# Low-rank adapter layer in float32: the left operand's rows put together by small SBUF transfers instead of a third transpose, with three steps reordered

## The reference, cut to what matters

```python
# x (2048, 1024); W_base (1024, 1024); A (16, 1024); B_user, B_item (1250, 1024, 16); W_common (1024, 16)
base = x @ W_base.T + b_base
a = x @ A.T                                       # (2048, 16)
user_part = einsum('bor,br->bo', B_user[user_indices], a)
item_part = einsum('bor,br->bo', B_item[item_indices], a)
common_part = a @ W_common.T
return base + 2.0 * (user_part + item_part + common_part)
```

## Time and profile before

| | us |
|---|---|
| runs | 217.42, 219.17, 219.26; median 219.17 |
| profiled execution, its time | 220.41 |
| its span, first to last instruction | 218.8 |
| PE busy | 207.4 |
| DVE busy | 167.3 |
| POOL busy | 73.6 |
| ACT busy | 57.4 |

### The profile page before, as it was taken

One profiled execution on the slowest core, in us unless ns is written; L12 is line 12 of the kernel. 1 busy time (PEld: TensorE's weight loads), 2 busy tenths in 40 slices (PEclk: granted clock), 3 DMA queues, 4 the chain that ended last, 5 costly groups with the idle time before them and its releaser, 6 DMA issues.

```text
span 218.8 us, 3157 instructions
## 1 busy us (share of the span) xinstructions
PE 207.4 (95%) x1176; PEld 180.6 (83%) x1176; DVE 167.3 (76%) x254; ACT 57.4 (26%) x95; POOL 73.6 (34%) x81
## 2 busy tenths in 40 slices
PE   7998999999997999999999999999999999999970
PEld 7787889888876989978889788988888888788870
DVE  1796899467799989999999999669995899136420
ACT  3688443331701232034101142036011400000000
POOL 6002181004052632415365164405441420178020
PEclk9999999999999999999999999999999999999997
DMA  6999969609859997788989989973899884226872
GB/s 196 381 413 402 265 208 319 261 1 252 360 162 318 353 321 267 269 304 311 316 300 298 366 317 258 380 283 123 298 307 366 332 306 173 99 71 217 192 133 63
DMA packets 14673, 57.77 MB, mean 264 GB/s; under 512 B 3812, under 2 KB 4196, under 8 KB 10668
## 3 DMA queue, kind: packets, MB, share of 16 engines
q0 software_dynamic: 7344, 35.30, 49.0%
q1 hardware_dynamic: 7024, 21.73, 27.8%
q10 hardware_dynamic: 288, 0.52, 0.7%
HBM read 58.95 MB, written 11.01 MB: 320 GB/s over the span
## 4 chain that ended last, share of the span: by engine, by line
PE 68%; DVE 16%; DMA 7%; SPq 3%; issue 1%; ACT 1%; DVEq 0%
PE main_ps L1082 17%; PE main_ps L1084 17%; PE main_ps L1083 17%; DVE acc L759 10%; DMA w_lo_raw<-w_t 5%; PE ps_a L1022 3%; PE main_ps L1152 3%; PE ps_a L1023 3%; PE ps_a L1024 3%; DMA x_lo_raw<-x_t 3%; DVE x_lo L655 2%; SPq L301 1%; PE main_ps L1145 1%; SPq L304 1%; PE main_ps L1123 1%
## 5 line engine op out<-in xcount | busy, mean ns | idle before, releaser
L759 DVE SCALAR_TENSOR_TENSOR acc<-rows,a_entry,acc 128x1024 f32<-128x1024 f32 x75 | 96.3, 1284 | 5.5 <-DMA rows<-table,fetch 3.5
L407 POOL DMA_INDIRECT rows<-table,fetch x40 | 54.0, 1349 | 100.8 <-DVE acc L759 90.6
L1082 PE MATMUL main_ps<-w_hi,x_hi 128*128 128x512 f32 (+1 forms) x224 | 83.9, 374 | 0.0
L1084 PE MATMUL main_ps<-w_hi,x_lo 128*128 128x512 f32 (+1 forms) x224 | 82.9, 370 | 0.0
L1083 PE MATMUL main_ps<-w_lo,x_hi 128*128 128x512 f32 (+1 forms) x224 | 82.7, 369 | 0.0
L1083 PEld LDWEIGHTS main_ps<-w_lo,x_hi 128*128 128x128 f32 x224 | 42.1, 188 | 5.5
L1082 PEld LDWEIGHTS main_ps<-w_hi,x_hi 128*128 128x128 f32 x224 | 42.1, 188 | 5.4
L1084 PEld LDWEIGHTS main_ps<-w_hi,x_lo 128*128 128x128 f32 x224 | 42.1, 188 | 4.8
L655 DVE TENSOR_TENSOR x_lo<-x_lo_raw,x_hi 128x1024 fp32r<-128x1024 f32 (+2 forms) x19 | 19.9, 1054 | 0.3
L536 ACT ACTIVATE out_sb<-main_ps 128x912 f32<-128x912 f32 x12 | 11.1, 930 | 33.1 <-PE main_ps L1084 31.2
L1022 PE MATMUL ps_a<-x_hi,w_hi 128*128 128x256 f32 x64 | 18.4, 287 | 0.6 <-DVE x_lo L655 0.3
(11 more groups left out here) (115 smaller groups left out, 166.1 us busy)
## 6 DMA issues: line engine op xcount, KB each, us to landing
out<-out_sb SPq DMA_DIRECT2D x15, 512.0 KB
x_lo_raw<-x_t SPq DMA_DIRECT2D x14, 512.0 KB, 8.1
w_lo_raw<-w_t SPq DMA_DIRECT2D x7, 512.0 KB, 7.4
x_lo_raw<-x_t SPq DMA_DIRECT2D x3, 256.0 KB, 5.8
rows<-table,fetch POOLq DMA_INDIRECT x40, 8.3
w_lo_raw<-w_t ACTq DMA_DIRECT2D x2, 256.0 KB, 4.0
set_sums<-acc SPq DMA_DIRECT2D x1, 512.0 KB, 3.2
out<-out_sb SPq DMA_DIRECT2D x2, 256.0 KB
```

Of the source, the lines that this page charges most:

```text
L407: pool.indirect_dma_start(out=rows[:, n % SLOTS, :], out_offset=None, in_=table_chunks, in_offset=bass.IndirectOffsetOnAxis(ap=fetch[:, s, ...
L759: return dve.scalar_tensor_tensor(to, rows_r, a_r, to, ALU.mult, ALU.add)
L1082: pe.matmul(to, x_hi[:, u % RING, k, x], w_hi[:, k, o], start=start, stop=False)
L1084: return pe.matmul(to, x_lo[:, u % RING, k, x], w_hi[:, k, o], start=False, stop=stop)
```

## The change

The table `left` and its transpose are gone. The two buffers of the third block of `low_t` are filled once (`put_left`) from a column `left_rows` of ones in each group's first 18 rows and zeros below. Then, per unit, ACT issues four transfers within SBUF after `copy_low`, each of 16 rows of 128 values (8 KB) from rows `4R:5R` of a turned block to the first 16 rows of a group. `left_of` waits for the semaphore of these transfers, no longer for the copy. Further: `left_of(0)`, `last_of(0)`, `last_of(1)` and `finish_first` come after `turn_low(1)`, one step of `base(2)` and `pack_entries(0)`; `make_x_hi(4, 0)` comes behind `first_part`, `second_part` and `spread_a` of unit 3, and `evacuate(2)` ahead of `make_x_hi(4, 1)`; `add_side(2)`, `add_side(3)` and the two `make_x_lo(6, ...)` come sooner among the row products; `add_to_out(2)` comes ahead of `bring_back()`.

```diff
-        left = sb("left", [P, LOW_RING, UT, 2, LEFT])
+        left_rows = sb("left_rows", [P, 1])
-        low_ps = ps_a[:, 0:NLT]
+        low_ps = ps_a[:, 0:UT * P]
...
             for q in range(UT * HALVES):
+                pool.memset(left_rows[q * LEFT:q * LEFT + BIAS_HI + 1, :], 1.0).then_inc(cleared, 1)
                 pool.memset(minus[q * LEFT:q * LEFT + BIAS_HI, :], -1.0).then_inc(cleared, 1)
...
+            add_to_out(2)
             bring_back()
-            add_to_out(2)
             add_to_out(3)
...
                 act.activation(low[:, u % LOW_RING, :, 4 * R:6 * R], split, ACT.Copy).then_inc(common_spread, 1)
-                act.activation(left[:, u % LOW_RING, :, :, 0:R], split[:, :, 0:R].unsqueeze(2).broadcast_to([P, UT, 2, R]),
-                               ACT.Copy).then_inc(common_spread, 1)
...
             def copy_low(u):
                 act.wait_ge(bank_a_filled, turn_a(f"lt{u}") + 1)
-                act.activation(low_t[:, u % LOW_RING, :], low_ps, ACT.Copy).then_inc(bank_a_taken, 1)
+                act.activation(low_t[:, u % LOW_RING, 0:UT * P], low_ps, ACT.Copy).then_inc(bank_a_taken, 1)
+                act.wait_ge(bank_a_taken, turn_a(f"lt{u}") + 1)
+                if u < LOW_RING:
+                    act.wait_ge(left_put, u + 1)
+
+                for j in range(UT):
+                    for half in range(HALVES):
+                        q = (j * HALVES + half) * LEFT
+                        act.dma_start(low_t[q:q + R, u % LOW_RING, UT * P:NLT].bitcast(f32),
+                                      low_t[4 * R:5 * R, u % LOW_RING, j * P:(j + 1) * P].bitcast(f32)).then_inc(left_ready[u % LOW_RING], 16)
+
+            def put_left(i):
+                act.wait_ge(cleared, 12)
+                act.activation(low_t[:, i, UT * P:NLT], left_rows[:, 0:1].broadcast_to([P, P]), ACT.Copy).then_inc(left_put, 1)
...
             copy_low(2)
-            make_x_hi(4, 0)
             first_part(3)
             second_part(3)
             spread_a(3)
+            make_x_hi(4, 0)
+            evacuate(2)
             make_x_hi(4, 1)
-            evacuate(2)
             copy_low(3)
...
             make_x_lo(4, 0)
+            add_side(2)
             row_products(0, range(4, 5))
-            add_side(2)
             make_x_lo(4, 1)
-            row_products(0, range(5, 7))
+            row_products(0, range(5, 6))
             take_rows(2)
             add_side(3)
-            row_products(0, range(7, CHUNKS))
+            row_products(0, range(6, CHUNKS))
...
             add_side(5)
+            make_x_lo(6, 0)
             row_products(1, range(7, CHUNKS))
-            row_products(2, range(0, 1))
-            make_x_lo(6, 0)
-            row_products(2, range(1, 2))
             make_x_lo(6, 1)
+            row_products(2, range(0, 2))
             take_rows(3)
...
             def turn_low(u):
                 pe.wait_ge(low_ready, 2 * (u + 1))
-                pe.wait_ge(common_spread, 2 * (u + 1))
+                pe.wait_ge(common_spread, u + 1)
                 my_bank_a(f"lt{u}")
                 for j in range(UT):
-                    pe.transpose(low_ps[:, j * P:(j + 1) * P], low[:, u % LOW_RING, j, :], ident[:, :])
-                done = pe.transpose(low_ps[:, UT * P:NLT], left[:, u % LOW_RING, :, :, :].rearrange("p t c r -> p (t c r)"),
-                                    ident[:, :])
+                    done = pe.transpose(low_ps[:, j * P:(j + 1) * P], low[:, u % LOW_RING, j, :], ident[:, :])
                 done.then_inc(bank_a_filled, 1)
...
                 pe.wait_ge(shared_lo, 2)
-                pe.wait_ge(bank_a_taken, turn_a(f"lt{u}") + 1)
+                pe.wait_ge(left_ready[u % LOW_RING], 16 * UT * HALVES * (u // LOW_RING + 1))
...
             turn_low(0)
             base(2, range(4, 5))
             pack_rows(1)
+            turn_low(1)
+            base(2, range(5, 6))
+            pack_entries(0)
             left_of(0, (False, False))
             last_of(0)
             last_of(1)
             finish_first(0).then_inc(tile_done, 1)
             finish_first(1).then_inc(tile_done, 1)
-            turn_low(1)
-            pack_entries(0)
-            base(2, range(5, 6))
             rank_a(3)
```

More of the change, by code:

```diff
@@ L252, in rec_kernel @@
         who_ready, rows_known, WHO_STEPS = sem("who_ready"), sem("rows_known"), 6
-        side_added = sem("side_added")
+        side_added, left_put = sem("side_added"), sem("left_put")
+        left_ready = [sem(f"left_ready{i}") for i in range(LOW_RING)]
         a_part_done, a_rest_ready = sem("a_part_done"), sem("a_rest_ready")
@@ L390, in _ @@
             pool.memset(left_raw, 0.0).then_inc(cleared, 1)
-            pool.memset(left[:, :, :, :, :], 0.0).then_inc(cleared, 1)
+            pool.memset(left_rows[:, :], 0.0).then_inc(cleared, 1)
             pool.memset(minus[:, :], 0.0).then_inc(cleared, 1)
@@ L394, in _ @@
             pool.wait_ge(cleared, 4)
-            for bias_row in (BIAS_LO, BIAS_HI):
-                pool.memset(left[:, :, :, :, bias_row:bias_row + 1], 1.0).then_inc(cleared, 1)
-            pool.wait_ge(cleared, 6)
             for q in range(UT * HALVES):
+                pool.memset(left_rows[q * LEFT:q * LEFT + BIAS_HI + 1, :], 1.0).then_inc(cleared, 1)
                 pool.memset(minus[q * LEFT:q * LEFT + BIAS_HI, :], -1.0).then_inc(cleared, 1)
@@ L433, in bring_back @@
                         bounds_check=P - 1, oob_is_err=False).then_inc(brought[t - FIRST_BACK], 16)
-            pool.wait_ge(cleared, 10)
+            pool.wait_ge(cleared, 12)
             pool.wait_ge(rows_known, 2)
@@ L512, in spread_a @@
                 act.wait_ge(a_split_ready, 2 * (u + 1))
-                if u == 0:
-                    act.wait_ge(cleared, 6)
                 if u >= LOW_RING:
@@ L571, in _ @@
             act.activation(left_w[:, :], left_raw, ACT.Copy).then_inc(shared_hi, 1)
+            for i in range(LOW_RING):
+                put_left(i)
             copy_at(0)
@@ L721, in spread_values @@
                 if u >= 2:
-                    dve.wait_ge(common_spread, 2 * (u - 1))
+                    dve.wait_ge(common_spread, u - 1)
                 split = a_split[:, u % 2, :, :]
@@ L854, in _ @@
             dve.wait_ge(shared_hi, 2)
-            dve.wait_ge(cleared, 10)
+            dve.wait_ge(cleared, 12)
             dve.scalar_tensor_tensor(left_w[:, :], left_w[:, :].bitcast(f32), minus[:, 0:1], left_raw,
```

## The result

The changed kernel is slower: 224.91 us at the median of 4 runs (224.09 to 226.12), against 219.21 of the kernel before on the same chip (217.42 to 219.59, 4 runs). The ratio is 1.026, with a 95% interval of 1.021 to 1.032. A ratio in this document counts only those runs of a kernel that are within 1.5% of its fastest, while a median and a range are over all its runs. The profiled execution took 225.12 us, its span is 223.5 us.

What follows compares the result with a forecast made beforehand. PE was taken to set the time. PE ending at -0.6 us plus -0.4 at the end gave -1.0 (profiled execution 220.41 to 219.4), or 218.2 us against the median 219.17; range 216.3 to 221.8.

Steps and rivals of the forecast that it cites:

- rival A: Transfers land late, so `left_of(0)` and `left_of(1)` wait: slower, up to 224.5 us; chance 0.17.
- B: PE's clock falls around the idle time at unit 0: +2.5 us if for 5 us, 220.7; chance 0.07.
- Third transposes: Eight third transposes leave PE's stream in `turn_low`, 0.11 us each: -0.88 us, all on the path.
- Issues of unit 0: ACT's four transfer issues after `copy_low(0)`: 0.32 us each, 1.27 in all, making `first_part(2)` 1.27 us late.
- rival D: Issues cost ACT 0.51 us each, 0.8 us later per unit: 219.0 us, no change, within the forecast's chance of 0.54.
- Landing of unit 0: Unit 0's transfers land in 2.0 us, at 44.7, so `left_of(0)` starts at 44.8: +2.14 us.
- Wait ahead of `rank_a(3)`: PE idles about 2.1 us for `copy_low(1)`, its cover used up; `rank_a(3)` starts at 49.1: +2.0 us.
- I take 3 us: Unit 1's transfers land in 3 us, between 2.0 and 8.1, with 3.8 us available: no wait at `left_of(1)`.
- The clock: PE's granted clock stays at 1.00 in 44 to 55 us, despite the idle time at unit 0.
- The reordered steps: DVE's earlier values remove PE's waits of 1.68 us at `left_of(2)` and 0.31 at `rank_a(6)`; nothing of DVE's late next.
- The end: Earlier `add_to_out(2)` gets `add_to_out(3)` out at about 202, so the last store lands sooner: -0.4 us.
- C: Smaller late start at unit 0 (0.45 us) and larger tail gain (1.1 us): faster, 216.6 us; chance 0.22.

Runs made afterwards that it cites:

- e5_pe_only: Kernel before with only PE's new order of unit 0 (`turn_low(1)`, a `base(2)` step and `pack_entries(0)` ahead of `left_of(0)`), no transfers: 220.78 us, ratio 1.011.
- e11_hold: Kernel after, with the first store, the two loads behind it and a gather held until unit 1's small transfers have landed: 224.3 us, no ratio given.
- after_again: The kernel after, unchanged, run and profiled again beside other runs of the kernel before: 228.04 us, ratio 1.037.
- e2_sides: Kernel before with only the reordered steps of ACT and DVE: 220.05 us, ratio 1.001.
- e3_both: Kernel before with the reordered steps of ACT and DVE and `add_to_out(2)` ahead of `bring_back()`, no transfers: 219.04 us, ratio 0.996.
- e8_sp_late: e3_both with third transposes kept for units 0 and 1, and transfers for units 2 to 7 issued by SP: 219.22 us, ratio 0.988.
- e1_tail: Kernel before with only `add_to_out(2)` moved ahead of `bring_back()`: 217.41 us, ratio 0.997.
- x_only: Kernel before with only the transfers and the shorter `copy_low`, every engine's order as before: 222.82 us, ratio 1.014.
- e14_x7: e8_sp_late with both halves of `x_lo(7)` one step sooner among DVE's products: 215.09 us, ratio 0.982 to the kernel before.

## Why the prediction was wrong

The forecast was 218.2 us with a range to 221.8, and 224.9 was measured, 3 us outside. It is rival A at unit 1 alone, with B inside it. That A's far end, 224.5, is so near is luck: it needs a landing of 4.0 us at unit 0 and of 8.1 at unit 1, where 2.2 and 7.6 were the longest. Step by step:

- **Third transposes, -0.88 us.** They are gone (1168 matmuls in place of 1176). The size is right: behind the start of `turn_low(4)` the next product starts after 0.13 us in the kernel after and after 0.25 before, behind that of `turn_low(5)` after 0.22 and 0.33. Only ahead of a wait, as at `turn_low(2)`, is it lost.
- **Issues of unit 0, 4 x 0.32 us.** Mis-sized. The nearest row was SP's issue of a transfer from memory; these take 0.61 us each on ACT, 2.48 in all. That is rival D and a bit more. `first_part(2)` came at 44.10 instead of 43.0, PE waited 1.33 us for the values at `pack_entries(0)`, and `left_of(0)` started at 45.64, not 44.8.
- **Landing of unit 0, 2.0 us.** Right: 1.8 to 2.2. The Trainium skill, DMA: Bandwidth & Descriptors, "Anatomy of one DMA", gives about 2.0 us as the fixed part of a transfer issued by GpSimd; these are issued by ACT, and the trace agrees in a quiet stretch. At unit 1 of the kernel after it doesn't.
- **Wait ahead of `rank_a(3)`, 2.1 us.** Right: 1.85, and 1.96 in e5_pe_only. The start is at 49.96, 0.86 off, which is the lateness of `left_of(0)` carried on.
- **"I take 3 us", the landing of unit 1.** This is the step that failed. It was 5.7 to 7.6 us. The bounds, 2.0 to 8.1, held it; the choice between them did not. Its reason, that small transfers with a queue of their own escape the crowd, is refuted by the pair of the kernel after (7.6 us) and e11_hold (1.7 us), which differ in the large transfers beside them. Its other reason, that the 8.1 us are mostly bytes, can hold for the queue ahead alone: the load's own are 1.2 us at the rate that the prediction uses. The row that argued for the upper end was in the prediction, a DMA share of 1.15 at 50 to 51 us. Besides, the slack of 3.8 us was counted to a last start at 50.0; it was at 51.7, of which 0.86 is unit 0's lateness and the rest three issues at 0.61 instead of 0.32. With 3 us of landing, 51.7 + 3 = 54.7 would have been before PE came at 56.25.
- **The clock.** Forecast at 1.00 in 44 to 55 us with a chance of 0.07 for B; it was 0.65 and 0.50 in 50 to 54. The prediction reasoned from a single gap of 1.68 us, but here two, 1.33 and 1.85 us, stand close together, a case that no row of before shows. e11_hold has the same fall without any later wait, after_again the same two gaps without a fall. The Trainium skill, TensorE: Matmul & The Clock Gate, "Why this matters for your kernels", was read as letting such gaps pass; after_again agrees, the kernel after and e11_hold do not, and there the measurement decides. For the time this fall was nothing, as it lay in a wait. The price is the second fall's, behind the wait for the landing: 1.54 us at `left_of(2)`.
- **The reordered steps.** The side wait at `left_of(2)` went, as said (no wait at 74.21; shown alone in e2_sides). "What is late next is nothing of DVE's" was wrong: `x_lo(7)` was next, for 1.04 and 3.29 us in the two profiles of the kernel after, 1.72 in e3_both and 2.50 in e8_sp_late.
- **The end, -0.4 us.** No effect of the edit that can be told from nothing (e1_tail). In the kernel after the last accumulating transfer was issued at 208.07 us, not ahead of 204, with everything else late as well. The profiled execution of before, 1.2 us over its median, had a tail that its other executions need not have had; taking its 4.1 us of landing as reducible was reading one draw.
- **The range.** Neither end follows from its terms: C's own sum gives 216.6, not 216.3, and A with 6.5 us at unit 1 and 4.0 at unit 0 is 220.9 + 2.0 = 222.9, not 221.8. The result lies above both.

With the two terms mis-sized put right the sum comes out by its own working: `left_of(1)` at 53.8 becomes 59.4, +5.6; the second fall of the clock +1.5; and 218.2 + 5.6 + 1.5 = 225.3, against 224.9. Up to `left_of(2)` the traces bear it out: 67.0 forecast, +5.6 and +1.5, and 74.21 measured. Behind that its nearness is luck. The last evacuation came 7.77 us later than before, where the sum has -0.6 + 7.1 = 6.5, because of the wait for `x_lo(7)`; and the tail behind it was 3.1 us shorter than in the trace before, where the sum has 0.4.

Why executions of one kernel differ by 2 to 6 us is open in the main. The two profiles of the kernel after (225.12 and 228.5 us) show one part: in the longer one DVE waited more for gathered rows, `make_x_lo(7, 1)` started at 146.43 us instead of 144.65, and PE's wait for it was 3.29 us instead of 1.04 with a fall of the clock behind it. The mean clock of a run is no measure of such stalls: in the profile of the kernel before it is 0.993, though the clock is at 1.00 from 36 to 212 us and falls only behind PE's last work, so a longer tail lowers it as well. The other kernels have one profile each, so what happened in their other runs isn't seen; in e2_sides this was enough to hide a gain of about 2 us that the profile shows. Open is also which waits of PE lower its clock (the list is below).

## What to carry to other kernels

A small transfer that replaces an operation on the bound engine is paid in issues (here 0.6 us each, with everything behind them in the queue) and in a landing that depends on what else starts at that time (1.8 us or 7.6): look up the large transfers that start within a microsecond of it, and where there are any, place it ahead of them or use it only where the slack exceeds the upper end. Work moved ahead to cover one wait uncovers another in full, and PE's waits can cost the clock as well, in one execution and not in the next. A fall of the clock ahead of a longer wait costs nothing, one behind it does (1.54 us here). A wait removed is worth only the distance to the next late value, so that one is to be looked up and brought forward in the same step.

## What the hardware did that was not expected

- Issuing an 8 KB transfer from SBUF to SBUF took 0.61 us on ACT and 0.59 us on SP, where SP's issue of 16 rows of 2 KB from memory took 0.32.
- The same transfer landed in 1.7 to 2.2 us in quiet and in 5.7 to 7.6 beside a store, two loads and a gather, with only 8 KB of its own.
- The length of PE's waits alone did not tell whether its granted clock fell. It fell to 0.50 behind two of 1.33 and 1.85 us close together in the kernel after (1.34 and 1.85 in e11_hold), and stayed at 1.00 behind 1.38 and 1.85 in after_again. It fell behind a single one of 2.82 us in x_only, and stayed at 1.00 behind one of 3.22 us ahead of 145.22 us in e11_hold, one of 2.50 in e8_sp_late and one of 1.68 in the kernel before.
- Runs of one kernel on one core spread over 2% and more, mostly in step with the mean granted clock of the run, but not always: the longest run of e14_x7, 217.25 us, had 1.000.
